# Attention on one core: the twelve looped pairs of heads written out, and a stage's sums copied out of PSUM in the division's order

## The reference

```
xf = groupnorm(x).reshape(2, 2048, 1024)
for Wq, Wk, Wv, lookahead in ((lb weights, False), (la weights, True)):      # 8 heads each, 64 wide
    q, k, v = xf @ Wq.T, xf @ Wk.T, xf @ Wv.T                                # per head
    s = where(mask, q @ k.T / 8, finfo.min)                                  # 2048 x 2048
    o.append(softmax(s) @ v)
o = concatenate(o, axis=1).reshape(2, 2048, 1024)                            # heads are not moved beside tokens
return x + o @ Wo.T
```

## Time and profile before

| | |
|---|---|
| median of 3 runs | 3242.12 us (3242.05 to 3242.49) |
| the profiled execution | 3242.84 us, its span 3241.0 us |
| busy | PE 3107.0 us (96%), DVE 1992.7 (61%), ACT 1600.2 (49%), POOL 1288.9 (40%) |
| attention | from about 1150 us to the end |

### The profile page before, as it was taken

One profiled execution on the slowest core, in us unless ns is written; L12 is line 12 of the kernel. 1 busy time (PEld: TensorE's weight loads), 2 busy tenths in 40 slices (PEclk: granted clock), 3 DMA queues, 4 the chain that ended last, 5 costly groups with the idle time before them and its releaser, 6 DMA issues.

```text
span 3241.0 us, 49178 instructions
## 1 busy us (share of the span) xinstructions
PE 3107.0 (96%) x14500; PEld 2513.5 (78%) x14500; DVE 1992.7 (61%) x3574; ACT 1600.2 (49%) x3188; POOL 1288.9 (40%) x1004
## 2 busy tenths in 40 slices
PE   6999999999999789999999999999999999999998
PEld 4788888888888567777777777877777777777786
DVE  6212313411211388877878778878887887788875
ACT  4210212211111066666666666666666666666665
POOL 4000001100000156555555556556565555565654
PEclk9999999999999799999999999999999999999999
DMA  4545735634433634333433234324433443344330
GB/s 141 167 128 146 221 115 138 185 117 102 141 116 96 142 79 107 77 72 72 97 86 71 66 85 98 78 66 96 94 72 69 95 90 72 68 96 90 72 72 21
DMA packets 352207, 325.17 MB, mean 100 GB/s; under 512 B 276225, under 2 KB 276225, under 8 KB 339713
## 3 DMA queue, kind: packets, MB, share of 16 engines
q1 hardware_dynamic: 352000, 323.02, 40.4%
HBM read 205.52 MB, written 117.44 MB: 100 GB/s over the span
## 4 chain that ended last, share of the span: by engine, by line
PE 56%; DVE 6%; issue 3%; DMA 0%; ACT 0%; DVEq 0%; SPq 0%; ACTq 0%
PE rows L1207 11%; PE max L1142 8%; PE scores L1175 7%; PE acc L1193 7%; PE acc L1189 7%; PE acc L1191 7%; PE scores L1170 7%; DVE o_full L1111 2%; DVE part_max L1063 1%; PE scores L1173 1%; PE side L1152 1%; DVE inv L1090 1%; DVE inv L1097 1%; DVE p_low L860 0%; DVE wo_l L1081 0%
## 5 line engine op out<-in xcount | busy, mean ns | idle before, releaser
L860 POOL TENSOR_TENSOR p_low<-probs,p_high 128x512 fp32r<-128x512 f32 (+2 forms) x960 | 1216.0, 1278 | 884.8 <-ACT p_high L996 815.0
L992 ACT ACTIVATE probs<-scores 128x512 f32<-128x512 f32 (+3 forms) x1280 | 684.0, 534 | 633.0 <-PE scores L1175 620.8
L1063 DVE TENSOR_REDUCE part_max<-max 128x1 f32<-128x512 f32 (+3 forms) x1280 | 764.5, 601 | 206.9 <-PE max L1142 176.5
L996 ACT ACTIVATE p_high<-scores 128x512 fp32r<-128x512 f32 (+3 forms) x1280 | 680.3, 531 | 0.0
L1142 PE MATMUL max<-k,q 128*128 128x512 f32 (+3 forms) x1280 | 483.5, 379 | 84.7 <-DVE part_max L1063 66.7
L418 DVE TENSOR_TENSOR stage_l<-proj,stage_h 128x512 fp32r<-128x512 f32 x192 | 132.0, 689 | 692.4 <-ACT stage_h L410 651.9
L410 ACT ACTIVATE stage_h<-proj 128x512 fp32r<-128x512 f32 x192 | 114.5, 598 | 830.2 <-PE proj L341 435.4
L1175 PE MATMUL scores<-q,k 128*128 128x512 f32 (+3 forms) x1280 | 490.8, 383 | 0.0
L1170 PE MATMUL scores<-q,k 128*128 128x512 f32 (+3 forms) x1280 | 472.7, 369 | 0.3 <-ACT p_high L996 0.3
L1193 PE MATMUL acc<-p_low,v 128*128 128x512 f32 (+3 forms) x1280 | 469.2, 367 | 0.0
L1189 PE MATMUL acc<-p_high,v 128*128 128x512 f32 (+3 forms) x1280 | 467.3, 365 | 0.9 <-DVE p_low L860 0.6
(11 more groups left out here) (93 smaller groups left out, 4322.2 us busy)
## 6 DMA issues: line engine op xcount, KB each, us to landing
qk_h<-stage_h SPq DMA_DIRECT2D x128, 256.0 KB, 2.6
qk_l<-stage_l SPq DMA_DIRECT2D x128, 256.0 KB, 3.0
q<-qk_h SPq DMA_DIRECT2D x64, 512.0 KB, 4.9
k<-qk_h SPq DMA_DIRECT2D x64, 512.0 KB, 6.8
xs<-xT SPq DMA_DIRECT2D x40, 512.0 KB, 4.9
w_raw<-wqk SPq DMA_DIRECT2D x32, 512.0 KB, 4.0
v_h<-stage_h SPq DMA_DIRECT2D x64, 256.0 KB, 2.6
v_l<-stage_l SPq DMA_DIRECT2D x64, 256.0 KB, 3.1
```

Source lines behind the costliest of these rows:

```text
L860: eng.tensor_tensor(p_low[:, n % 4, part], probs[:, n % 4, part], p_high[:, n % 4, part].bitcast(F32), ALU.subtract).then_inc(done, 1)
L992: nc.scalar.activation(probs[:, n % 4, 0:cols], scores[n % 2][:, 0:cols], ACT.Exp, scale=SCALE).then_inc(exp_done, 1)
L996: nc.scalar.activation(p_high[:, n % 4, 0:cols], scores[n % 2][:, 0:cols], ACT.Exp, scale=SCALE).then_inc(high_act, 1)
L1063: nc.vector.tensor_reduce(part_max[:, s % 2, at, m:m + 1], max_bank[n % 2][:, 0:cols], AX.X, ALU.max).then_inc(max_read, 1)
```

## The change

`pairs` calls the body 16 times in Python, so every engine gets 16 pairs of straight code and no loop. And `leave` reads the bank with a step of 16 elements and writes `acc_s` as a run, in the order `(a j r)`, so that the two operands of each division are runs of 256 elements. The transposes and the reciprocal work on the new order unchanged; `o_full` is written as before, in 8 runs of 32.

```
-            body(0, LB, LB)
-            with eng.Fori(1, PAIRS // 2 - 1) as i:
-                body(i, LB, LB)
-            body(PAIRS // 2 - 1, LB, LA)
-            body(PAIRS // 2, LA, LA)
-            with eng.Fori(PAIRS // 2 + 1, PAIRS - 1) as i:
-                body(i, LA, LA)
-            body(PAIRS - 1, LA, None)
+            for i in range(PAIRS):
+                after = i + 1 - (i + 1 == PAIRS)
+                body(i, LB if i < PAIRS // 2 else LA,
+                     None if i + 1 == PAIRS else LB if after < PAIRS // 2 else LA)
...
-                    nc.scalar.activation(acc_s[:, :], acc[n % 2][:, :], ACT.Copy).then_inc(acc_copied, 1)
+                    nc.scalar.activation(acc_s[:, :].rearrange("p (a j r) -> p a j r", a=2, j=JP),
+                                         acc[n % 2][:, :].rearrange("p (r j a) -> p a j r", j=JP, a=2),
+                                         ACT.Copy).then_inc(acc_copied, 1)
...
-                        sums, by = (x.rearrange("e (r j a) -> e a j r", j=JP, a=2)[:, a]
+                        sums, by = (x.rearrange("e (a j r) -> e a j r", j=JP, a=2)[:, a]
```

## The result

| | before | after |
|---|---|---|
| median of 4 runs, us | 3242.30 | 3198.22 |
| lowest to highest, us | 3242.05 to 3254.02 | 3197.83 to 3212.86 |
| profiled execution, its span, us | 3242.84, 3241.0 | 3198.25, 3196.5 |
| heads 1 to 30 in the trace, us | 1947.49 | 1904.17 |

The ratio is 0.9861, with a 95% interval from 0.9837 to 0.9885. The forecast was 3199 us.

A forecast was written before the change was run, and what follows sets the result against it. PE, busy 3107 of 3241 us, was taken as the bound, with only its idle time to save. 3242.84 - 31.2 (loops) - 11.8 (division) = 3199.8, less 0.72 for the median: 3199 us; 8-in-10 range 3176 to 3213.

The forecast's parts named there:

- Writing out the loops: Both attention loops as straight code: 21.7 us from the first and 9.6 from the second, 31.2 us together.
- The rival that straight code would make DVE wait: Straight code makes DVE wait 1.91 us in each of 16 pairs; only the division's gain stays, 3230 us; chance 0.05.
- Pricing by the pair: Loop gain from pair lengths with branches (132.07, 129.65 us) and without (127.74), holding idle time and slow clock together.
- The division: DVE's multiplications on runs take 0.41 us instead of 0.60; PE's wait per head falls 0.38, 11.8 us over 31 heads.
- the rival in which the whole wait goes: At head starts POOL no longer comes between the two multiplications; 31 x 1.08 = 33.5 us saved, 3177 us; chance 0.13.
- The rival of no gain: The division gives PE nothing: the step was not the cost, or POOL's turn fills the gap; 3211 us; chance 0.17.
- The copy on ACT: ACT's stepped copy into `acc_s` takes 0.97 us instead of 0.60, covered by ACT's waits; cost nothing.
- The cover of 1.13 us: Room at a head's start from the copy's begin to ACT's next exponential, including 0.52 us waiting for PE.
- the copy that the prediction doubled: ACT's copy doubled to 1.2 us by 8-byte PSUM lines, 0.07 past the room; sum 3201; 1.2 to 2.5 us: 0.06.
- The sum: Profiled 3242.84 us less 31.2 and 11.8 gives 3199.8; the median lies 0.72 below, 3199 us.

The follow-up runs named there:

- straight_only: The kernel before with the pairs written out on every engine, copy and division unchanged; 3211.86 us, ratio 0.9895 to before.
- looped_dve: The kernel before with the loops written out on all engines but DVE, copy and division unchanged; 3242.93 us, ratio 0.9988 to before.
- pool_short: The changed kernel with POOL computing only the first 64 columns of each of its low parts; 3156.07 us, ratio 0.9731 to before.
- one_stepped: The changed kernel with the division reading `inv` at the old step, `acc_s` still a run, result not the reference; 3212.76 us in 1 run.

## Why the prediction was right

**Writing out the loops (31.2).** Right: straight_only gave 32.7 in 30 heads. Nearly all of the 1.5 more is the pace: its pairs take 127.65 where the six heads of the earlier trace rows that it was priced by took 127.74, 0.09 for each of 15 pairs, 1.35. The rival that straight code would make DVE wait has no row for it, since no wait on issue is left. The prediction named DVE's branch alone; the experiments add that ACT's stood hidden behind it, worth more than half as much by itself. Pricing by the pair took both in, and the lower clock with them. Counting DVE's waits takes in neither; that they add up to 33.6 us, near the 32.7, is chance. What the prediction said first, that only PE's idle time can go, was too narrow: PE's busy time fell by 12.7 us too, in part by the clock, and the pairs held that as well. The Trainium skill, "Runtime: NRT & Kernel Launch", section "Instruction fetch mechanics", says that code is fetched ahead in sequence, and that a taken branch out of what has been fetched must wait for its target. The traces agree: 2.63 and 2.25 us behind a branch, none in straight code, and one late instruction instead of two when the code was shifted. In each of these waits a packet on an instruction queue starts (looped_dve); that it held the late instruction no record says.

**The division (11.8).** Right in mechanism and nearly in size. Alone it takes 0.404 us at the least (0.41 was taken), at a head's start the pair takes 2.32 (2.3), PE waits 0.72 (0.70). In 30 heads it is 10.6 us (1914.76 - 1904.17) against 30 x 0.38 = 11.4. That POOL keeps its turn between the two is shown by pool_short, where both together take 0.94; the rival in which the whole wait goes could not come while POOL had work there. The rival of no gain fell with one_stepped: the step is the cost, since with `inv` alone stepped, and the output as it was, the 0.58 us are back.

**The copy on ACT (nothing).** Right that it costs nothing, but the estimate of its length was wrong: 0.97 was taken, 0.602 measured, as before the change (0.603). The prediction carried the division's price over to another engine and another memory; ACT's copy out of PSUM doesn't show the step. The cover of 1.13 us that was to hide it wasn't needed. So the rule of the Trainium skill that spoke against the copy ("Advanced Engine Details and Errata", "PSUM Cachelines") doesn't reach it: the copy that the prediction doubled would have taken 1.2 us, and the 128 copies lie between 597 and 608 ns. For the matmuls that the page names, no run here shows it.

**The sum.** 31.2 + 11.8 = 43.0 us, 44.6 by the profiled execution: 43.3 in heads 1 to 30, the rest outside them, where runs of one kernel differ by more than that. That the sum is so close is in part luck: in the 30 heads the loops gave 1.5 us more than was reckoned and the division 0.8 less.

## What to carry to other kernels

Price a loop's branch by the length of an iteration with and without it, where the trace has both, rather than by the waits of one engine: several engines branch at once and hide one another, and the clock's share appears in no wait. When an operation has to read with a step, let the engine that doesn't pay for it do so, and look at every operand of the engine that does: with one of two left stepped, almost nothing was gained. Where two engines take turns by whole instructions, shortening one's instruction gives back only its own part; moving it behind what the bottleneck waits for gave more here (0.42 us per head, against 0.35 for making both multiplications a third shorter), until it was moved one step too far.

## What the runs showed of the hardware

- A step of 64 bytes on 64x256 elements of SBUF costs DVE's multiplication 0.19 us (0.595 against 0.404), and with `inv` alone stepped it still takes 0.58. The same step in ACT's read of 128x512 out of PSUM costs nothing (602 against 603 ns).
- The price of the same branch hangs on where the code lies: 120 fulfilled waits added to DVE's code made the 30 heads 12.0 us shorter, and most of that was the clock, which no longer fell to the lower level in the first loop (1.00 instead of 0.98).
- Behind a branch DVE's late instructions came 1.9 to 2.8 us late, and a packet of 8 KB on an instruction queue started within each such wait (14 in the kernel before, 9 in looped_dve).
- DVE's multiplication and POOL's instruction take turns whole: every contended one of the kernel after (129) ends 0.27 to 0.29 us behind an instruction of POOL.
- PE was shown as busy for 62.72 us of a head whose 310 products take 62.29 without a stop. A listed wait of 0.70 to 0.75 us moved the next two products by 0.97 to 1.01 in all.
